# A graph-and-mixer network on one core: edge sums without ring copies, and the first feed-forward network tile by tile inside the fourth graph layer

## The reference, cut to what matters

```python
# block 0, graph network, four times (gnn0); X is the state
h = einsum('ni,rio->rno', X, W)                 # the tables: 4 x 6250 rows of 256
agg = segment_sum(h[etype, src] * inv_deg, dst) # the edge sums
out = agg + X @ root + bias
X = elu(layernorm(out)) + X
# block 0, mixer: linear attention and a two-layer network with norms, from x (rows "first_x")
# block 0, feed-forward (ffn0)
y = first_x + X
z = layernorm(y)
s = z @ wr + br                                 # one score per node, kept for the selection
base = y + z
new = (gelu(z @ w1 + b1) @ w2 + b2) * s         # 256 -> 1024 -> 256
# then: the nodes with the highest scores take `new` on top of `base` (select, tables1)
```

## Time and profile before

| | us |
|---|---|
| median of 3 runs | 7984.36 (7972.84 to 7988.71) |
| profiled execution, its own time | 7983.88 |
| span in its profile | 7982.1 |

### The profile page before, as it was taken

One profiled execution on the slowest core, in us unless ns is written; L12 is line 12 of the kernel. 1 busy time (PEld: TensorE's weight loads), 2 busy tenths in 40 slices (PEclk: granted clock), 3 DMA queues, 4 the chain that ended last, 5 costly groups with the idle time before them and its releaser, 6 DMA issues. The chain is left out here.

```text
span 7982.1 us, 89847 instructions
## 1 busy us (share of the span) xinstructions
PE 5806.8 (73%) x17886; PEld 3446.9 (43%) x17886; DVE 4250.2 (53%) x14583; ACT 2839.0 (36%) x7998; POOL 4226.4 (53%) x4288
## 2 busy tenths in 40 slices
PE   0488888878777777777778888786597777763398
PEld 0244444444444444444433333454344444442265
DVE  7216665657776666666656666323434666642412
ACT  0134444434444455555533333221123443421122
POOL 0017777767777666666667777200004777743211
PEclk9799999888998888899966555797798787876699
DMA  1444444444444444444443333100244333320000
GB/s 57 140 137 132 132 131 131 131 135 143 144 143 142 139 129 128 127 129 128 129 133 105 105 105 105 49 0 0 75 136 125 106 106 106 106 72 1 13 14 18
DMA packets 479425, 815.31 MB, mean 102 GB/s; under 512 B 88660, under 2 KB 343208, under 8 KB 478716
## 3 DMA queue, kind: packets, MB, share of 16 engines
q0 software_dynamic: 200480, 548.02, 24.0%
q1 hardware_dynamic: 278488, 262.51, 10.0%
HBM read 614.04 MB, written 196.16 MB: 102 GB/s over the span
## 5 line engine op out<-in xcount | busy, mean ns | idle before, releaser
L537 POOL DMA_INDIRECT gnn_msg<-tables,gnn_row_ring x4165 | 4003.6, 961 | 1900.2 <-issue 1513.9
L585 PE MATMUL bank<-gnn_msg,gnn_hot 128*128 128x256 f32 x8330 | 3117.4, 488 | 861.9 <-DVE sums L566 559.5
L566 DVE TENSOR_TENSOR sums<-sums,bank 128x256 f32 x4165 | 1746.7, 419 | 1821.1 <-PE bank L585 1145.2
L585 PEld LDWEIGHTS bank<-gnn_msg,gnn_hot 128*128 128x128 f32 x8330 | 1709.2, 232 | 2262.4 <-issue 1256.8
L134 POOL TENSOR_TENSOR ve<-mv,eps 128x7 f32<-128x7 f32 x35 | 7.2, 205 | 1349.7 <-DVE mv L128 1201.9
L527 ACT ACTIVATE gnn_hot<-gnn_away,gnn_meta_ring 128x128 f32<-128x128 f32 x1568 | 645.9, 482 | 47.3 <-ACT gnn_meta_ring L518 0.8
L696 PE MATMUL bank<-gnn_w,residual 128*128 128x512 f32 x1176 | 646.1, 634 | 0.0
L515 ACT ACTIVATE gnn_away<-iota,gnn_meta_ring 128x128 f32<-128x128 f32 x1960 | 625.0, 390 | 25.3 <-DMA residual<-in_L_mix_b_dram 14.0
L546 DVE TENSOR_SCALAR gnn_hot<-iota,gnn_meta_ring 128x128 f32<-128x128 f32 x1764 | 620.0, 352 | 0.5 <-ACT gnn_meta_ring L503 0.5
L502 ACT COPY gnn_row_ring<-row 128x9 int32<-128x9 int32 x490 | 95.0, 194 | 798.2 <-PE bank L585 786.2
L670 ACT ACTIVATE gnn_own<-gnn_own 128x256 f32<-128x256 f32 x196 | 81.6, 416 | 800.8 <-DVE gnn_own L650 800.8
(11 more groups left out here) (389 smaller groups left out, 6524.4 us busy)
## 6 DMA issues: line engine op xcount, KB each, us to landing
tables<-residual SPq DMA_DIRECT2D x294, 256.0 KB, 2.8
gnn_msg<-tables,gnn_row_ring POOLq DMA_INDIRECT x4165, 2.7
tables<-sums SPq DMA_DIRECT2D x98, 512.0 KB, 2.9
tables<-gnn_msg SPq DMA_DIRECT2D x98, 256.0 KB, 2.1
residual<-first_norm_columns SPq DMA_DIRECT2D x98, 128.0 KB, 4.0
first_norm<-state SPq DMA_DIRECT2D x1, 6272.0 KB, 22.2
first_rows<-residual SPq DMA_DIRECT2D x1, 6272.0 KB, 39.1
residual<-first_norm SPq DMA_DIRECT2D x49, 128.0 KB, 3.8
```

Of the source, the lines that this page charges most:

```text
L537: self.nc.gpsimd.indirect_dma_start(out=self.msg[:, s0 + u, :], out_offset=None, in_=table, in_offset=bass.IndirectOffsetOnAxis(ap=self.ro ...
L566: self.nc.vector.tensor_tensor(at, at, self.sums(s, phase), ALU.add).then_inc(self.added, 1)
L585: self.nc.tensor.matmul(self.sums(s, phase), self.hot[:, s, :], self.msg[:, s, :], start=True, stop=True).then_inc(self.summed, 1)
```

## The change

It has two parts.

*Edge sums.* The ring and its copies are gone. GpSimd, ScalarE and VectorE read row numbers, local rows and weights where they lie for all steps; the negated weights are made once, in `edge_tables`. Each gather waits for the matmul that used its buffer one body ago. ScalarE makes the one-hot matrices of the odd slots, VectorE those of the nine even ones. ScalarE makes both halves for the next body. VectorE has two sets of 18 registers and loads the next body's after slot 11.

*Feed-forward network.* The stage `ffn0` goes. A class `Ffn0` runs it tile by tile as hooks in layer 4: the rows of the tile of the body before are summed in slots 9 to 11, the tile before that goes through norm, score, both products and out. The 6.3 MB reload becomes 49 loads of one tile. `res` and `agg` change names after `gnn0`, since the base is now written into the sums.

```diff
-HALVES = ((0, 9), (9, 8))
+SCALAR_SLOTS = ((1, 3, 5, 7), (9, 11, 13, 15))
+VECTOR_SLOTS = tuple(s for s in range(SLOTS) if not any(s in part for part in SCALAR_SLOTS))
+TILES_AT = 11
...
+    def gpsimd(self, pool, n, table):
+        for s in range(SLOTS):
+            if n:
+                pool.wait_ge(self.summed, (n - 1) * SLOTS + s + 1)
+            at = n % NT * SLOTS + s
+            self.nc.gpsimd.indirect_dma_start(
+                out=self.msg[:, s, :], out_offset=None, in_=table,
+                in_offset=bass.IndirectOffsetOnAxis(ap=self.rows[:, at:at + 1], axis=0)).then_inc(self.landed[s], 16)
...
     def scalar_hots(self, act, n, h):
...
+        c, slots, made = self.c, SCALAR_SLOTS[h], (2 * n + h) * len(SCALAR_SLOTS[0])
+        if n:
+            act.wait_ge(self.summed, (n - 1) * SLOTS + slots[-1] + 1)
...
+    def vector(self, dve, n, after, last=False):
+        tiles = self.tiles
         for s in range(SLOTS):
+            dve.wait_ge(self.summed, n * SLOTS + s + 1)
+            if n or s:
+                dve.wait_ge(self.added, n * SLOTS + s)
+            at = self.c.agg[:, ds(tiles[s] * D, D)]
+            self.nc.vector.tensor_tensor(at, at, self.sums(n, s), ALU.add).then_inc(self.added, 1)
+            if s in VECTOR_SLOTS and not last:
+                self.one_hot(n + 1, s)
+            after(s)
+            if s == TILES_AT and not last:
+                self.tiles = body_tiles(dve, self.c, n + 1)
...
+class Ffn0:
...  # sum_rows (VectorE, tile j): slot 9 u = xs + x, slot 10 bn_stats, slot 11 bn_aggr
...  # vector (tile j): slot 3 shift, slot 5 product with wr and its sum, slot 6 the score twice, slot 7 base = u + hat
+            if s == 7:                       # tensor, tile j
+                pe.wait_ge(self.s_hat, j + 1)
...
+                for h in range(KH):
+                    ins = t.transpose(c.bank[3][:, h * P:(h + 1) * P], self.hat[:, h * P:(h + 1) * P], c.ident[:])
+            if s in (8, 9, 10, 11):
+                b = (s - 8) // 2
+                if s == 8:
+                    pe.wait_ge(self.s_xt, j + 1)
...
+                for m in (2 * (s - 8), 2 * (s - 8) + 1):
+                    for h in range(KH):
+                        ins = t.matmul(c.bank[b][:, (m - 4 * b) * P:(m - 4 * b + 1) * P], self.w1[:, h, m * P:(m + 1) * P],
+                                       self.xt[:, h, :], start=(h == 0), stop=(h == KH - 1))
...
+            if s == 14:                      # one row of bias, 256 columns
...
+            if s in (15, 16):
+                pe.wait_ge(self.s_act, 8 * j + 4 * (s - 14))
+                for m in range(4 * (s - 15), 4 * (s - 15) + 4):
+                    ins = t.matmul(c.bank[2][:, 0:D], self.ht[:, m, :], self.w2[:, m, :], start=False, stop=(m == 7))
...
 # gnn0, layers 1 to 3, ScalarE
                         post.exponential(act, n)
-                        edges.ring(act, i + 1, n + 1, 0)
-                        edges.scalar_hots(act, n, 1)
+                        edges.scalar_hots(act, n + 1, 0)
                         post.turned(act, n, t)
-                        edges.scalar_hots(act, n + 1, 0)
                         post.way_out(act, n, 0)
-                        edges.ring(act, i + 1, n + 1, 1)
+                        edges.scalar_hots(act, n + 1, 1)
                         post.way_out(act, n, 1)
 # gnn0, layer 4, ScalarE
+                act.wait_ge(ffn.s_in, 7 * 16)
+                for i in range(1, NT + 2):
+                    n = i + LASTL * NT
+                    if i > 2:
+                        ffn.out(act, i - 3, ranked_tile(act, c, i - 3))
+                    if i > 1:
+                        ffn.norm(act, i - 2)
+                    if i < NT + 1:
+                        post.exponential(act, n)
+                    if i > 1:
+                        ffn.turned(act, i - 2)
+                    if i < NT - 1:
+                        edges.scalar_hots(act, n + 1, 0)
+                    if i > 1:
+                        for b in range(2):
+                            ffn.hidden(act, i - 2, b)
+                    if i < NT - 1:
+                        edges.scalar_hots(act, n + 1, 1)
 # gnn0, layer 4, SyncE
-                sp.wait_ge(post.s_out, LASTL * NT * 2 + 2)
-                sp.dma_start(c.res[:].rearrange("p (t d) -> p t d", d=D), c.x_d.rearrange("(t p) d -> p t d", p=P)).then_inc(s_res, 16)
-                sp.wait_ge(s_res, 16)
+                ffn.begin_sync(sp, a)
+                for j in range(NT):
+                    ffn.load(sp, j, ranked_tile(sp, c, j))
 # gnn0, layer 4, TensorE
+                pe.wait_ge(ffn.s_in, 7 * 16)
+                for i in range(NT):
+                    edges.tensor(pe, i + LASTL * NT, ffn.tensor(pe, i - 2) if i > 1 else nothing)
+                for j in (NT - 2, NT - 1):
+                    drain(ffn.tensor(pe, j))
...
-            ffn0(nc, c, a, score)
             select(nc, c, score, take)
```

More of the change, by code:

```diff
@@ L492, in sums @@
[L492 to L503, removed]
@@ L505, in scalar_hots @@
-    def scalar_hots(self, act, n, h):
[L507 to L515, removed]
-                .then_inc(self.away_ready, 1)
[L517 to L523, removed]
-            u = DVE_HOTS[h] + k
-            to = self.hot[:, s0 + u, :]
+        self.hot_ready, self.away_ready, self.act_hot_ready, self.summed, self.added = (
+            c.sem(n) for n in ("hot_made", "distances_made", "scalar_hot_made", "steps_summed", "steps_added"))
@@ L557, in vector @@
-    def vector(self, dve, tiles, n, phase, after, last=False):
-        for h, (s0, w) in enumerate(HALVES):
-            for u in range(w):
-                s = s0 + u
-                t = tiles[s]
-                dve.wait_ge(self.summed, n * SLOTS + (SLOTS + s + 1))
-                dve.wait_ge(self.added, n * SLOTS + (SLOTS + s))
-                at = self.c.agg[:, ds(t * D, D)]
-                self.nc.vector.tensor_tensor(at, at, self.sums(s, phase), ALU.add).then_inc(self.added, 1)
-                if not (last and h == 1):
-                    hots = NEXT_HOTS[h][u]
-                    if hots and hots[0] == 0:
-                        dve.wait_ge(self.ring_ready, n * 4 + (2 * h + 4))
-                    for k in hots:
-                        self.one_hot(1 - h, k)
-                after(s)
@@ L575, in tensor @@
-    def tensor(self, pe, n, phase, after):
-        for s in range(SLOTS):
-            pe.wait_ge(self.landed[s], n * 16 + 16)
-            h = 0 if s < HALF else 1
-            u = s - HALVES[h][0]
-            if u < DVE_HOTS[h]:
-                pe.wait_ge(self.hot_ready, n * sum(DVE_HOTS) + (h * DVE_HOTS[0] + u + 1))
-            else:
-                pe.wait_ge(self.act_hot_ready, n * 2 * ACT_HOTS + (h * ACT_HOTS + u - DVE_HOTS[h] + 1))
-            pe.wait_ge(self.added, n * SLOTS + (SLOTS + s - SUM_SLOTS + 1))
-            self.nc.tensor.matmul(self.sums(s, phase), self.hot[:, s, :], self.msg[:, s, :], start=True, stop=True).then_inc(self.summed, 1)
+                bias, scale = c.ones[:, 0:1], -1.0
@@ new lines, in tensor @@
+    def tensor(self, pe, n, after):
+        for s in range(SLOTS):
+            if s in VECTOR_SLOTS:
+                pe.wait_ge(self.hot_ready, n * len(VECTOR_SLOTS) + VECTOR_SLOTS.index(s) + 1)
+            else:
+                made = [u for part in SCALAR_SLOTS for u in part]
+                pe.wait_ge(self.act_hot_ready, n * len(made) + made.index(s) + 1)
+            if n * SLOTS + s >= SUM_SLOTS:
+                pe.wait_ge(self.added, n * SLOTS + s - SUM_SLOTS + 1)
+            pe.wait_ge(self.landed[s], n * 16 + 16)
+            self.nc.tensor.matmul(self.sums(n, s), self.hot[:, s, :], self.msg[:, s, :], start=True, stop=True).then_inc(self.summed, 1)
@@ L586, in tensor @@
             after(s)
-def each_body(eng, first, last, body):
-    for i in range(first, last):
-        body(i, i)
 def both(*hooks):
```

427 lines of the change are left out of this document (216 added, 211 removed).

## The result

The changed kernel takes 7582.44 us in the median of four runs (7578.96 to 7584.80), the kernel before in the same session 7980.11 us (7972.84 to 7988.71). The ratio is 0.9501 with a 95% interval of 0.9484 to 0.9517. The forecast was 7486 us, its range 7385 to 7640: direction and range held, but the gain is 398 us where 498 were forecast. The profiled execution took 7578.96 us and its span is 7577.2 us, 404.9 less than the span before.

A forecast was written before the change was run, and what follows sets the result against it. GpSimd's gather issue was taken to bound layers 4 and 5, a chain through TensorE, VectorE and ScalarE layer 3. -440 + 56 + 5 - 21 - 24 - 75 = -499 gave about 7486 us, range 7385 to 7640.

The forecast's parts named there:

- The stage and its tail: Between last edge addition and selection: the 473.2 us stage goes, a 33 us tail for the last tiles comes; -440 us.
- Layers 1 and 2: First two layers: bodies fall to 21.7 us, near the gathers' floor; 1085 us each, -21 and -24 us.
- Layer 3: Third layer: a shorter chain through TensorE, VectorE and ScalarE brings 24.6 us per body to 22.85; -75 us.
- The load's share: Layer 3's chain: moving VectorE's register load behind slot 11 gains 1.3 us per body; bounds 0 and 2.6.
- waits at slot 15 for the base: Edge sums: TensorE needs at slot 15 the base VectorE writes in slot 14; about 2.3 us per two bodies stay.
- Rival D: Waits only cost: chain keeps its pace in layers 1 to 3, GpSimd pays 17 ns per gather; 7634 us, chance 0.04.
- Layer 4: Layer carrying the network behind its gathers: body 22.5 instead of 21.36 us, +56 us, and +5 us for weights.
- the wait for the network's weights: Start of layer 4: all three engines wait for the weights; +5 us, bounds 0 and +12.
- Slots 8 to 11, 1.5 us each: Layer 4's body: the first product with the edge matmuls takes 1.5 us in each of these slots.
- took 0.9 for the layer: TensorE's clock in the new layer 4, taken from layer 3's 0.90; layer 4 had 0.60 before.
- The reading of the chain: Layer 4's body: VectorE's slot 5, ScalarE's exponential, copy of transposed rows, first product, slot 11 follow in turn; 7.8 us.
- rival A: All at the gathers' pace: layer 3 at 21.7 us per body, layer 4 near 21.5; 7382 us, chance 0.18.

The follow-up runs named there:

- the experiment with halves: The changed kernel with gathers waiting twice a body, as the ring copies made them, instead of one by one: 7573.8 us.
- part 1 only: The changed kernel with only the new edge sums and register load; the feed-forward network stays a separate stage, layer 4 as before: 7859.1 us.
- keep busy: The changed kernel with three unread 128x256 products added per layer 4 body, behind the transposes at slot 7: 7500.4 us.
- the best version: The changed kernel with ScalarE's copy ahead of the exponential in layer 4, register load behind slot 8 in layers 1 to 3, slot 11 in layer 4: 7383.4 us.

## Why the prediction was right, and where it was wrong

*The stage and its tail* (-440): -442, the tail 30.8 us where 33 were worked out. *Layers 1 and 2*: as forecast, at the gathers' floor; the experiment with halves adds that the form of the wait had not held them, which leaves the ring copies' lateness. *Layer 3* (-75): -86. The load's share was taken as 62 us and measures 58.6; 28 us are left for the ring copies and the looser waits together, where 22 were forecast. How they share it stays open. TensorE waits at slot 15 for the base in all three layers as the working said (45.5, 85.9 and 42.7 us, L660 for L628). Rival D, 17 ns for each gather, is refuted: all gaps at the floor are 0.30 us as in the earlier trace rows, and layer 4 of "part 1 only" is 2 us longer, not 14.

*Layer 4* (+61) is the failed step: +177. Of the +61, the wait for the network's weights was put at 5 us, and it cost 7: the layer's first addition starts 16.5 us behind its first gather, before the change 9.5. The miss is in the body: the sum had 22.5 us, and the steady bodies take 25.2; the text's own bound for a wrong forecast was 25. Its terms against the means over bodies 10 to 47:

| term of the body, us | forecast | even, odd bodies |
|---|---|---|
| VectorE's slots 0 to 5 | 6.9 | 6.8, 6.7 |
| slot 5 to slot 11: exponential, copy, first product | 7.8 | 9.9, 10.4 |
| register load, to slot 12 | 5.9, 2.9 | 5.3, 2.8 |
| slots 12 to 16 | 2.6 | 2.6, 2.8 |
| next slot 0 | 0.9 | 0.9, 2.2 |
| sum | 24.1, 21.1 | 25.5, 24.8 |

All terms but two fit within 0.6 us. "Slots 8 to 11, 1.5 us each" took 2.7, 2.1 and 1.4 us from one to the next. The working had both prices in hand, 1.05 and 1.91 us for a group of eight, and it named the wait of 2.9 us ahead of the product; it then priced the product at the high clock and took 0.9 for the layer. So the path through slot 11 was mis-sized: the wait was put in as time, and the product behind it at a clock that it did not get: "keep busy" gives back 1.7 us per body, most of the 2.3 us by which the term was short. The last term, 2.2 instead of 0.9 in odd bodies, is VectorE catching up with a late TensorE behind a short load, and waiting for it.

The reading of the chain was right, since moving the copy ahead took away every stall. But the order in ScalarE's queue was treated as given: one exchange of two calls brings layer 4 to rival A's pace. That the best version measured 7383 where A said 7382 is partly luck. A has layer 3 at the gathers' pace too, some 1096 us, and it took 1119; other layers made up for it.

Open is what holds layer 3 above the floor with the load at slot 8; it still stalls 24 us there, at slots 13 to 16. Of the -11 us from the selection on, 8 lie behind the last gather of layer 5. All kernels with the new edge sums have the same code there and take 863 to 875 us for it, the kernel before 872, so no gain of the change is shown in them.

## What to carry to other kernels

When a stage's work is spread behind another's, list for each in-order queue what stands ahead of the one instruction that the busiest engine waits for; a table load and two activations ahead of a 0.35 us copy cost this kernel 2%. Price a wait of TensorE twice, as its own length and as the work behind it at the low clock, and look at the sparse work ahead of it too, since here the clock mostly fell before the long wait began. A few useless matmuls in the wait are a cheap test of which of the two you pay: if the kernel gets faster with them, look for a wait to take away, which here was worth twice as much (166 us against 82).

## What the runs showed of the hardware that was not expected

With three added products in each body (2.77 us of TensorE's time in the one shown) the kernel ran 82 us faster. TensorE's mean clock in layer 4 was 0.57 with the edge sums alone, 0.83 with the network in the order of the change, 0.89 with the added products and 0.95 with the earlier copy.

A register load of 18 words took 1.6 us or 4.1 us in layer 4, by the row's address alone: shifting the table by 8 bytes exchanged which rows were slow.

A wait before each of 4165 gathers on GpSimd in place of two waits a body did not lengthen the 0.30 us between gathers.
